# A mixture of experts and three convolution layers on one core: the transposes back to rows start two tasks later, and one high part goes ahead of a read

## The reference

```python
outs = [_causal_dwconv(x_flat, w) for w in (w3, w7, w15)]
y = jnp.concatenate(outs, axis=1)
y = y.reshape(b, h, n_scales * d, l).transpose(0, 3, 1, 2)
return jnp.einsum('blhm,dm->blhd', y, w_mix)
```

## Time and profile before

| | us |
|---|---|
| median of 3 runs | 1070.13 (1069.55 to 1070.31) |
| the profiled execution's own time | 1071.84 |
| its span, first to last instruction | 1070.2 |
| TensorE matmuls busy | 1007.4 (94%) |
| VectorE busy | 491.7 (46%) |
| ScalarE busy | 318.3 (30%) |
| GpSimd busy | 189.5 (18%) |
| mean granted TensorE clock, share of full speed | 0.969 |

### The profile page before, as it was taken

The page is one execution under the profiler, slowest core; times in us unless marked ns, Lnnn a source line. Parts: engine busy times, 40 slices in busy tenths (PEclk is TensorE's granted clock), DMA queues, the critical chain, the costliest instruction groups (busy, mean ns, idle before and its releaser), DMA issues.

```text
span 1070.2 us, 14224 instructions
## 1 busy us (share of the span) xinstructions
PE 1007.4 (94%) x5089; PEld 842.3 (79%) x5090; DVE 491.7 (46%) x658; ACT 318.3 (30%) x435; POOL 189.5 (18%) x229
## 2 busy tenths in 40 slices
PE   5569999999999999999999999968999999996998
PEld 3267888888888888888888888858888988895787
DVE  4772245146116336116336154156635893588011
ACT  2412244144125234125244144122401230122113
POOL 2030212112111212111212111111400231023100
PEclk9859999999999999999999999979999999998999
DMA  9563115962981894981994985981566367634557
GB/s 397 241 241 136 31 29 191 393 220 81 405 318 29 338 390 137 409 305 28 352 392 138 408 290 230 362 270 60 175 202 192 110 206 209 184 110 138 179 159 213
DMA packets 84864, 238.05 MB, mean 222 GB/s; under 512 B 8544, under 2 KB 50656, under 8 KB 69920
## 3 DMA queue, kind: packets, MB, share of 16 engines
q1 hardware_dynamic: 76608, 214.54, 53.9%
q0 software_dynamic: 8080, 23.07, 9.1%
q10 hardware_dynamic: 144, 0.02, 0.0%
HBM read 129.86 MB, written 111.94 MB: 226 GB/s over the span
## 4 chain that ended last, share of the span: by engine, by line
PE 69%; DMA 12%; DVE 10%; issue 3%; SPq 3%; ACT 2%; POOL 0%; DVEq 0%; ACTq 0%; POOLq 0%
PE gate_ps L965 13%; PE up_ps L965 13%; DMA w_raw<-in_w13T 10%; PE y_ps L952 9%; PE head_ps L1481 7%; PE head_ps L1485 7%; PE head_ps L1482 7%; PE y_ps L955 4%; SPq L442 3%; PE hT_ps L974 2%; DVE scaled L1275 1%; DVE split L1285 1%; PE xT_ps L942 1%; PE xT_ps L883 1%; PE head_ps L1493 1%
## 5 line engine op out<-in xcount | busy, mean ns | idle before, releaser
L1481 PE MATMUL head_ps<-split,ring 128*128 128x256 f32 (+1 forms) x525 | 182.6, 348 | 1.1 <-ACT split L1170 1.0
L965 PE MATMUL gate_ps<-front 128*128 128x512 f32 x560 | 177.3, 398 | 2.3 <-DVE xT_lo L819 1.4
L1485 PE MATMUL head_ps<-split,ring 128*128 128x256 f32 (+1 forms) x525 | 178.3, 340 | 1.1 <-DVE split L1285 1.0
L1482 PE MATMUL head_ps<-split,ring 128*128 128x256 f32 (+1 forms) x525 | 177.5, 338 | 0.0
L965 PE MATMUL up_ps<-front 128*128 128x512 f32 x560 | 173.6, 392 | 0.0
L834 DVE TENSOR_TENSOR hidden<-silu,up_ps 128x1024 f32<-128x1024 f32 x35 | 42.7, 1221 | 239.1 <-ACT silu L620 239.1
L965 PEld LDWEIGHTS up_ps<-front 128*128 128x128 f32 x560 | 105.8, 189 | 22.3
L965 PEld LDWEIGHTS gate_ps<-front 128*128 128x128 f32 x560 | 103.0, 190 | 23.5 <-DVE front L783 2.1
L620 ACT ACTIVATE silu<-gate_ps 128x1024 f32<-128x1024 f32 x35 | 35.9, 1024 | 270.5 <-PE up_ps L965 270.5
L952 PE MATMUL y_ps<-w_hi,hT_hi 128*128 128x512 f32 x280 | 112.4, 401 | 1.2 <-ACT hT_hi L602 1.2
L1485 PEld LDWEIGHTS head_ps<-split,ring 128*128 128x128 f32 x525 | 100.4, 191 | 13.4 <-DVE split L1285 1.7
(11 more groups left out here) (187 smaller groups left out, 1286.1 us busy)
## 6 DMA issues: line engine op xcount, KB each, us to landing
filters<-rows SPq DMA_DIRECT2D x56, 1568.0 KB, 18.4
w_raw<-in_w13T SPq DMA_DIRECT2D x32, 1024.0 KB, 6.4
w_raw<-in_w2T SPq DMA_DIRECT2D x16, 1024.0 KB, 6.2
ring<-filters SPq DMA_DIRECT2D x15, 1024.0 KB, 6.3
ring<-filters SPq DMA_DIRECT2D x18, 640.0 KB, 4.7
ring<-filters SPq DMA_DIRECT2D x18, 512.0 KB, 4.4
ring<-filters SPq DMA_DIRECT2D x33, 256.0 KB, 3.3
ring<-filters SPq DMA_DIRECT2D x96, 64.0 KB, 4.8
```

The source lines that it names most:

```text
L965: last = nc.tensor.matmul(o[:, n, :], a[:, k, :], b[:, k, t, n * 512:(n + 1) * 512], start=(k == 0 and a is xT_hi and b is w13_hi), stop=( ...
L1481: nc.tensor.matmul(place, kernel_hi, x_hi, start=(u == 0 and a == 0), stop=False)
L1482: nc.tensor.matmul(place, kernel_lo, x_hi, start=False, stop=False)
L1485: nc.tensor.matmul(place, kernel_hi, x_lo, start=False, stop=False)
```

## The change

In the first convolution layer, ScalarE's `high(0, 2)` is issued ahead of `take_stream(3)` instead of behind it. In the last, the calls of `unturn` inside `between` move:

| task | before, ahead of group 1 / 2 | after, ahead of group 1 / 2 |
|---|---|---|
| 5 | - / 0 | - / - |
| 6 | 1 / 2 | - / - |
| 7 | 3 / 4 | 0 / 1 |
| 8 | 5 / 6 | 2 / 3 |
| 9 | 7 / - | 4 / 5 |
| 10 | 8 / - | 6 / 7 |
| 11 | 9 / - | 8 / 9 |
| 12 to 21 | task - 2 / - | task - 2 / - |

The two transposes behind the last head (tasks 20 and 21) stay.

```diff
--- before.py
+++ after.py
@@ -1193,9 +1193,11 @@
             lane_roots(0)
             take_stream(0)
             for i in range(HALVES):
-                if i + 1 < HALVES:
+                if i + 1 < HALVES and i != 2:
                     take_stream(i + 1)
                 high(0, i)
+                if i == 2:
+                    take_stream(i + 1)
             lane_roots(1)
             take_stream(HALVES)
             for i in range(HALVES, len(PIECES)):
@@ -1517,10 +1519,10 @@
                 if l and k == 0:
                     total(l, 4 + u)
                 if l == LAYERS - 1:
-                    if u == 1 and k >= 9:
+                    if u == 1 and k >= 12:
                         unturn(n - 2)
-                    elif k < 9 and 2 * k + u >= 12:
-                        unturn(n - k + (2 * k + u - 12))
+                    elif 7 <= k < 12:
+                        unturn(n - k + 2 * (k - 7) + u - 1)
 
             def first_turns(pair):
                 turn(HALVES * pair)
```

## The result

| us | before | after |
|---|---|---|
| median of 4 runs | 1070.22 (1069.55 to 1070.39) | 1058.49 (1057.47 to 1058.94) |
| the profiled execution's own time | 1071.84 | 1057.47 |
| its span | 1070.2 | 1055.8 |
| mean granted TensorE clock | 0.969 | 0.975 |

The ratio of the times is 0.9881, with a 95% interval of 0.9869 to 0.9894: faster by 11.7 us; 11.6 were forecast, and 1058.5.

A forecast was written before the change was run, and what follows sets the result against it. TensorE was taken to bound the kernel almost everywhere, so only its idle time and clock count. The terms 10.98 and 0.65 us sum to 11.6 us, giving a median of 1058.5 us, range 1056.7 to 1061.

The forecast's parts named there:

- The stall of the third transpose: Last layer, task 6: moving the transpose that waits for ScalarE's first placement removes wait and half clock, 10.98 us.
- What is late next: Last layer, tasks 7 to 11: pieces, casts, filters, placements and stores all come in time after the move; cost 0.
- Rival B: Last layer: the pieces become the bound and part of the stall returns in smaller waits; 1061.9 us, chance 0.07.
- part 1: First layer: high(0, 2) ahead of take_stream(3) cuts TensorE's 0.85 us wait for the fourth piece to 0.20; 0.65 us.
- Rival C: Last layer: TensorE waits as long for the last low part, only part 1 stays; 1069.5 us, chance 0.02.
- D: End of kernel: the ninth placement slips and delays the stores, making it slower, in the extreme 1077 us; chance 0.02.
- The clock in the first layer: Fall to 1.2 GHz near 735 us, behind the statistics chain: could move some tenths, at most 1.5 us.
- the sum: Whole kernel: 10.98 + 0.65 = 11.6 us saved, taking the profiled execution from 1071.84 to 1060.2 us.
- The clock behind the stall: Last layer: half clock lasting 3 to 7 us in the median's runs changes the saving by 0.7 less to 1.4 more.

The follow-up runs named there:

- e3: Kernel before with the last layer's transposes shifted one task later instead of two, first layer unchanged; 1063.76 us, ratio 0.9932.
- e11: Changed kernel with the transposes one task later again, two each in tasks 8 to 13; 1059.18 us, ratio 0.9896 to the kernel before.
- e4: Kernel before, TensorE's order untouched, ScalarE's placements 0 to 2 issued behind high parts 17 to 19 of the last layer; 1060.90 us, ratio 0.9902.
- e6: Changed kernel once more, nothing altered, for a second profile; 1058.10 us.
- e7: Changed kernel with VectorE's deviations of the third and fourth batch ahead of both subtractions in the first layer; 1058.39 us, ratio 0.9886 to the kernel before.
- e8: Kernel before with the moved transposes and the reordered deviations of e7, but high(0, 2) still behind take_stream(3); 1059.54 us, ratio 0.9899.
- e9: Changed kernel once more, timed beside e10 on the same chip; 1059.52 us, ratio 0.9896 to the kernel before.
- e10: Kernel before with only the last layer's transposes moved, as in e2, timed beside e9; 1060.55 us, ratio 0.9907.
- e2: Kernel before with only the last layer's transposes moved to tasks 7 to 11, first layer unchanged; 1059.05 us, ratio 0.9890.
- e1: Kernel before with only high(0, 2) issued ahead of take_stream(3), transposes unchanged; 1070.12 us against 1070.80, ratio 0.9991.
- e5: Kernel before once more, nothing altered, for a second profile; 1071.72 us.

## Why the prediction was right, and where it was not

**The stall of the third transpose (10.98 us): right, cause and size.** S2 fell by 10.94. e3 shows that what counts is where the third transpose stands against ScalarE's last high part (one task gives back all but 2.45 us of waiting and 1.7 of clock), e11 that a third task adds nothing to two, and e4 that ScalarE's order was the cause, not TensorE's. The best number came from a control in the same trace: the twin task of the layer before gave 9.92 us, and the changed kernel has 9.92.

**What is late next: nothing, right.** Rival B had pieces as the new bound; no wait of the lines for the high and low parts in tasks 6 to 9 is in the profile after, and S2 agrees to 0.2 us over the change, e4, e6, e7, e8, e9, e10 and e11 (75.80 to 75.99). e2 has 76.17. Against e10, the same kernel, its surplus of 0.18 is there at the first matmul on `shared` (2.40 us behind the addition that opens S2, against 2.23) and no larger at the end, so it lies in how early that addition came and not in a loss on TensorE. The cast that part 1 moves, for which rival B allowed a collision, starts at 717.40 and takes 1.28; VectorE has nothing to do from 717.25 to 719.86, so nothing meets it. Rival C needed an operand that tasks 6 to 8 don't read. Of D, late stores, nothing is there: SyncE comes to them at 1034.78, 14.4 us earlier than before, as everything else, and from the last addition to the end it is 5.48 us, 5.52 before.

**Part 1 (0.65 us): right in size, incomplete in effect.** At the same state of the clock, part 1 is worth 0.60 to 0.62 (38.82 in e10 against 38.20 to 38.22 in the change, e9 and e11). With the fall it is 40.18 to 40.34 against 39.47, 0.7 to 0.9. Each comparison has a single profile on one side, e10 and e6. The median of runs resolves this badly: 0.7 in e1 and 1.0 between e9 and e10, both inside their noise. TensorE's remainder was 0.23 where 0.20 was forecast.

**The clock in the first layer: mis-sized.** The prediction let the fall at 735 us move by some tenths, and bounded it at 1.5. It did not move in the changed kernel's first profile, it was absent: S1 gained 1.98, of which 0.6 is the step and some 1.3 the clock. That is 1.3 of the 2.7 us by which the profiled time of 1057.47 lay under the 1060.2 that the sum gave; the other 1.4 are the experts, where nothing had changed. Over the profiles in which nothing else was changed in the first layer, the fall is in five of six without part 1 (before, e2 to e5; not e10) and in one of five with it (e6; not the change, e1, e9 or e11). That leans to part 1 making it rarer. Eleven executions don't settle it. Nor does the idleness of this stretch alone say when it comes: e8 waited 0.86, 0.27, 0.57 and 0.85 us between 724 and 737 and has the fall, e10 waited 0.59, 1.47 and 0.78 and has not. It stays open.

**The clock behind the stall.** I allowed 3 to 7 us of lower clock; the executions show 4.3 (before), 3.6 (e5, the same kernel) and 6.0 (e1, the same last layer), and in S2 that is 86.82, 86.46 and 87.56. None shows the 7. The Trainium skill, page "TensorE: Matmul & The Clock Gate", section "What's actually happening", which the prediction cited, states of the start of a kernel that the number of slow matmuls varies from run to run; behind this stall the first two agree with it, by 0.7 us.

That the median hit 1058.5 to 0.1 us is partly luck: the same two kernels are 11.4 us apart in the batch of e9, and single executions of one kernel spread over 1.5 us (the changed one, first batch) to 4.1 us (e10).

## What to carry to other kernels

When a program for several engines is written by hand, a helper that reuses a buffer waits for its consumer's place in another engine's program, not for the consumer's work: look up what stands ahead of that consumer before putting the helper among critical work. A stall on TensorE is priced from a twin of the same work elsewhere in the trace, which includes the clock's share. Small terms are read from stages cut at fixed events in profiles with the same state of the clock; totals of single executions don't carry them.

## What was unexpected of the hardware

A wait of 2.45 us, the only one in its stretch, was followed by 3.4 us at 1.2 GHz (e3). So was one of 1.5 us in the first layer in six of the eleven profiles that have it, and in e8 there was none above 0.86 us in that stretch and the clock fell all the same. Nor does one kernel always do the same: the changed kernel fell to 0.50 in e6 and stayed at 1.00 in e9. With the fall the stage takes 1.3 us more (39.47 against 38.20), in a kernel that is otherwise unchanged. The stage ahead of the convolution layers varied by 3.5 us (709.3 in e2, 712.8 in e4) although all these kernels are the same there.
